# Attention scores of two sequences in one burst, and four instructions moved within a turn

## The reference, cut to what matters

```python
for i in range(DEPTH):                       # 6 layers
    x = attn_layer(shift_tokens(x), ...) + x
    x = ffn_layer(shift_tokens(x), ...) + x
# attn_layer, 16 heads of 64, window 32
q = l2norm(q) * qs; k = l2norm(k) * ksc      # then rotary, with a scale by position
sim = einsum('bhwie,bhwje->bhwij', q, k of own and previous window) * 8
sim = where(mask, -max, sim); attn = softmax(sim)
out = einsum(attn, v); return out @ Wo
# ffn_layer
xn = layernorm(x) * g + bln
a, gate = split(xn @ W1 + b1); return a * gelu(gate) @ W2 + b2
```

## Time and profile before

| | us |
|---|---|
| median of 3 runs | 3596.83 (3594.86 to 3598.45) |
| the profiled execution, its own time | 3596.09 |
| span of its trace | 3594.3 |
| PE busy | 3394.7 (94%) |
| DVE busy | 3151.4 (88%) |
| ACT busy | 2999.4 (83%) |
| POOL busy | 2877.3 (80%) |

### The profile page before, as it was taken

How to read it: one execution, slowest core, us unless ns; L and a number is a source line. 1 busy time by engine, 2 the same in 40 slices (tenths; PEclk the granted TensorE clock), 3 DMA queues, 4 the chain that set the end, 5 groups by cost and what they waited for, 6 DMA issues and landing times.

```text
span 3594.3 us, 92498 instructions
## 1 busy us (share of the span) xinstructions
PE 3394.7 (94%) x29710; PEld 2110.8 (59%) x29710; DVE 3151.4 (88%) x10872; ACT 2999.4 (83%) x8812; POOL 2877.3 (80%) x2383
## 2 busy tenths in 40 slices
PE   7887999999999999999999999999999999999998
PEld 3444656656666666666656666666666656666665
DVE  7998988988988888988988988988988988988986
ACT  6554888888888888888888888888888888888887
POOL 6887887888887888887888887888887888887883
PEclk9998999999999999999999999999999999999999
DMA  5443322333323333322333322333332333332332
GB/s 164 141 133 124 113 99 102 108 115 108 115 101 101 106 112 106 116 103 99 107 115 107 116 102 99 110 116 103 115 106 96 108 118 105 114 106 99 106 103 92
DMA packets 261726, 396.22 MB, mean 110 GB/s; under 512 B 45566, under 2 KB 86588, under 8 KB 261244
## 3 DMA queue, kind: packets, MB, share of 16 engines
q1 hardware_dynamic: 261244, 390.30, 32.4%
HBM read 157.91 MB, written 6.03 MB: 46 GB/s over the span
## 4 chain that ended last, share of the span: by engine, by line
PE 53%; DVE 17%; POOL 14%; issue 7%; ACT 6%; DMA 2%; SPq 1%; DVEq 0%; POOLq 0%; ACTq 0%
PE bank L886 9%; PE bank L875 7%; PE bank L847 6%; PE bank L360 5%; PE bank L362 5%; PE bank L361 5%; DVE ab L1610 4%; PE bank L914 4%; PE bank L829 4%; POOL rot L1359 4%; POOL pr L1345 4%; PE bank L856 4%; DVE wide L1502 3%; PE bank L857 3%; DVE sm L1655 2%
## 5 line engine op out<-in xcount | busy, mean ns | idle before, releaser
L1184 ACT ACTIVATE pr<-sm,nb,rq 128x128 f32<-128x128 f32 (+1 forms) x3072 | 1518.0, 502 | 10.8 <-DVE nb L1661 10.7
L1345 POOL TENSOR_TENSOR pr<-pr,rden 128x640 f32<-128x640 f32 x768 | 966.2, 1258 | 460.1 <-DVE rden L1635 457.7
L1359 POOL TENSOR_TENSOR rot<-ab,swp 128x512 f32<-128x512 f32 x760 | 978.0, 1287 | 74.0 <-DMA swp<-ab 73.4
L1610 DVE TENSOR_TENSOR ab<-bank,ltab 128x1024 f32<-128x1024 f32 x760 | 925.1, 1217 | 80.6 <-PE bank L362 66.7
L1655 DVE CUSTOM_DVE_ANT_0 sm<-bank,mask 128x128 f32<-128x128 f32 (+1 forms) x3072 | 839.4, 328 | 47.5 <-PE bank L847 42.1
L1184 ACT ACTIVATION_READ_ACCUMULATOR pr<-sm,nb,rq 128x1 f32 x3072 | 599.5, 195 | 0.0
L847 PEld LDWEIGHTS bank<-rot 64*64 64x64 f32 x12288 | 288.1, 132 | 436.0 <-issue 364.7
L1365 POOL TENSOR_TENSOR rot<-rot,rkb 128x512 f32<-128x512 f32 x384 | 492.3, 1289 | 64.3 <-DMA rkb<-k_scratch 64.1
L1642 DVE COPY pt<-bank 128x512 f32<-128x512 f32 x768 | 531.3, 692 | 10.2
L875 PE MATMUL bank<-pt,vtok 128*64 128x160 f32 (+1 forms) x6144 | 461.6, 292 | 29.4 <-ACT vtok L1198 29.4
L1172 ACT ACTIVATE sq<-bank 128x512 f32<-128x512 f32 x768 | 452.6, 589 | 43.2 <-DVE ab L1610 19.9
(11 more groups left out here) (213 smaller groups left out, 5743.7 us busy)
## 6 DMA issues: line engine op xcount, KB each, us to landing
swp<-ab SPq DMA_DIRECT2D x1520, 128.0 KB, 2.0
rkb<-k_scratch SPq DMA_DIRECT2D x768, 128.0 KB, 2.9
rot<-c_scratch SPq DMA_DIRECT2D x64, 256.0 KB, 3.3
sq<-c_scratch SPq DMA_DIRECT2D x64, 256.0 KB, 3.3
xs<-xT SPq DMA_DIRECT2D x95, 128.0 KB, 2.3
xs<-xT SPq DMA_DIRECT2D x95, 127.5 KB, 2.4
raw<-Wqkv SPq DMA_DIRECT2D x48, 128.0 KB, 2.7
wo<-Wo SPq DMA_DIRECT2D x6, 512.0 KB, 4.6
```

Of the source, the lines that this page charges most:

```text
L1184: ins = act.activation(pr[:, s % 4, i, t, 0:P + WINDOW * t], sm[:, s % 2, i, cs], ACT.Exp, bias=nb[:, s, t, i:i + 1], scale=head_scale(rq, ...
L1345: ins = pool.tensor_tensor(pr[:, e % 4, :, :, :], pr[:, e % 4, :, :, :], rden[:, e, :, :].rearrange("p t i -> p i t").unsqueeze(3) .to_bro ...
L1359: pool.tensor_tensor(rot[:, PAIRS * (j % 2) + j // 2, :], ab_of(j, 0, lead), swp_of(j, lead), ALU.add).then_inc(qk_rot, 1)
L1610: dve.tensor_tensor(ab_both(j, lead).rearrange("p i (b t) -> p i b t", b=GB), seqs(qk_bank(j, lead)[:, :]).unsqueeze(1).to_broadcast(shape ...
```

## The change

1. `scores` is called in even steps alone and computes both sequences of the head pair in one burst of 16 small matmuls; each sequence has its own 256 columns of banks 0 and 1. The first of the four tiles of a sequence has 64 columns in place of 96. The burst waits for the bias of both sequences of the pair before.
2. PE calls `outputs` right behind `scores`, ahead of the down, output and centring products.
3. DVE takes all maxima of a pair in the even step, in the order: both heads of the first sequence, head 0 of the second, the bias of the first, head 1 of the second. The bias of the second sequence is made in the odd step, ahead of `copy_probs`. The maxima go to the new tile `mx` in SBUF; before they went to spare columns of bank 1.
4. In `copy_probs` one small transpose for two steps of probabilities stands in the even step, and waits for `normalise` of both.
5. Moved in a turn: the layer norm's logarithm and exponential on ACT from step 8 to step 9; `scale_q` of `next` on DVE from 11 to 12; `scale_k` of pair 7 on POOL from 13 to 12; and `a` 0 and `a` 1 exchange their banks (6 and 4).

```diff
@@ tables
- [..., ('prev', 'a', 0, 6), ('next', 'sum', 1, 7), ('prev', 'a', 1, 4)],
+ [..., ('prev', 'a', 0, 4), ('next', 'sum', 1, 7), ('prev', 'a', 1, 6)],
+ 'ln_n': 9,
- 'scale_q': (11, 4),
+ 'scale_q': (12, 4),
-SCALE_STEPS = {13: [('cur', 7)],
+SCALE_STEPS = {12: [('cur', 7)],
-SCORE_TILES = [(0, 0, 0), (1, 32, 32), (2, P, P - WINDOW), (3, P + 64, P + 32)]
+SCORE_TILES = [(0, 64), (32, 96), (P - WINDOW, 96), (P + 32, 96)]
@@ PE
-                def scores(s):
...
-                    if b == 0:
-                        pe.wait_ge(k_norm, scaled)
-                    pe.wait_ge(sc_bias, used)
+                def scores(p):
+
+                    pe.wait_ge(k_norm, n8 + (p + 1))
+                    pe.wait_ge(sc_bias, n16 + 2 * p)
+                    for b in range(GB):
+                        c0 = b * SEQ
+                        for m, (k0, count) in enumerate(SCORE_TILES):
...
-                    if cur is not None:
-                        scores(s)
+                    if s % 2 == 0 and cur is not None:
+                        scores(s // 2)
+                    if s % 2 == 0 and s < 6 and prev is not None:
+                        outputs(s, s // 2 + 5, prev)
+                    if s % 2 == 0 and s >= 6 and cur is not None:
+                        outputs(s, s // 2 - 3, cur)
                     bank_work(s, ("dn", "wo", "rqT", "cen"))
@@ ACT
-                    if s == AT["ln_k"] and (nxt is not None or prev is not None) and kind != "drain":
-                        norms(0, nxt, prev)
+                    if s == AT["ln_k"] and nxt is not None and kind != "drain":
+                        norms(0, nxt, None)
+                    if s == AT["ln_n"] and prev is not None and kind != "drain":
+                        norms(0, None, prev)
@@ DVE
-                    dve.transpose(pt[96:128, e % 4, :, 0, P:P + WINDOW], pr[0:32, e % 4, :, 1, 0:WINDOW])
+                    if e % 2 == 0:
+                        both = slice(e % 4, e % 4 + 2)
+                        dve.wait_ge(p_norm, n16 + (16 * q + e + 2))
+                        dve.transpose(pt[96:128, both, :, 0, P:P + WINDOW], pr[0:32, both, :, 1, 0:WINDOW])
...
+                    if s % 2 and cur is not None:
+                        bias(s)
...
-                    if cur is not None:
-                        maxima(s)
+                    if s % 2 == 0 and cur is not None:
+                        maxima(s, (0, 1))
+                        maxima(s + 1, (0,))
+                        bias(s)
+                        maxima(s + 1, (1,))
```

More of the change, by code:

```diff
@@ L74 @@
  [('prev', 'g', 0, 4), ('next', 'qk', 12, 5)], [('prev', 'g', 1, 6), ('next', 'qk', 13, 5)],
- [('prev', 'g', 2, 7), ('next', 'qk', 14, 5), ('prev', 'a', 0, 6), ('next', 'sum', 1, 7), ('prev', 'a', 1, 4)],
+ [('prev', 'g', 2, 7), ('next', 'qk', 14, 5), ('prev', 'a', 0, 4), ('next', 'sum', 1, 7), ('prev', 'a', 1, 6)],
  [('prev', 'a', 2, 6), ('next', 'qk', 15, 5)]]
@@ L190, in build @@
         nb = sb("nb", [P, STEPS, 2, 2])
+        mx = sb("mx", [P, 2, 2, 2])
         den = sb("den", [P, STEPS, 2, 2])
@@ L203, in build @@
         wide_f = wide[:, :, :].rearrange("p a n -> p (a n)")
-        mx = bank[1][:, UW:UW + 4].rearrange("p (t i) -> p t i", t=2)
         pt_f, pr_f = (t[:, :, :, :, :].rearrange("p a b c d -> p (a b c d)") for t in (pt, pr))
@@ L832, in square_sums @@
                     mm.then_inc(sq_part, 1)
-                def scores(s):
-                    p, b = s // 2, s % 2
-                    scaled = (n8 + (p + 1))
-                    used = (n16 + s)
-                    if b == 0:
-                        pe.wait_ge(k_norm, scaled)
-                    pe.wait_ge(sc_bias, used)
-                    c0 = b * SEQ
-                    for half, c, k0 in SCORE_TILES:
-                        part = slice(64 * (half % 2), 64 * (half % 2) + 64)
-                        for i in range(2):
-                            rows = slice(64 * i, 64 * i + 64)
-                            mm = pe.matmul(bank[i][part, c:c + 96], rot[rows, p, c0 + 64 * half:c0 + 64 * half + 64],
-                                           rot[rows, PAIRS + p, c0 + k0:c0 + k0 + 96], start=True, stop=True)
+                def scores(p):
[4 more added lines that the diff above has]
+                        for m, (k0, count) in enumerate(SCORE_TILES):
+                            part = slice(64 * (m % 2), 64 * (m % 2) + 64)
+                            for i in range(2):
+                                rows = slice(64 * i, 64 * i + 64)
+                                mm = pe.matmul(bank[i][part, c0 + k0:c0 + k0 + count],
+                                               rot[rows, p, c0 + 64 * m:c0 + 64 * m + 64],
+                                               rot[rows, PAIRS + p, c0 + k0:c0 + k0 + count], start=True, stop=True)
                     mm.then_inc(sc_ps, 1)
@@ L973, in turn @@
                         project_out(s - AT["wo"], prev)
-                    if s % 2 == 0 and s < 6 and prev is not None:
-                        outputs(s, s // 2 + 5, prev)
-                    if s % 2 == 0 and s >= 6 and cur is not None:
-                        outputs(s, s // 2 - 3, cur)
                     if s < 3 and prev is not None:
@@ L1660, in maxima @@
                         dve.wait_ge(rq_sb, n2 + (s // 8 + 1))
-                    dve.tensor_tensor(nb[:, s, :, :], mx, head_scale(nrq, p, b), ALU.mult).then_inc(sc_bias, 1)
+                    dve.tensor_tensor(nb[:, s, :, :], mx[:, b, :, :], head_scale(nrq, p, b), ALU.mult).then_inc(sc_bias, 1)
                 def clamp(h, q):
```

17 lines of the change are left out of this document (10 added, 7 removed).

## The result

The changed kernel takes 3717.32 us (median of 4 runs, 3712.45 to 3723.2), the kernel before 3597.64 (4 runs, 3594.86 to 3600.67). The ratio is 1.0334, 95% interval 1.0319 to 1.0350: it is slower by 120 us, where 71 us faster was forecast. The time lies above the range, and beyond the slower rival's 3634.

A forecast was written before the change was run, and what follows sets the result against it. PE was taken to set the pace in part A, ACT's chain in part B. Part A loses 1.52 us a turn, part B stays; over 47 stretches that is 71 us, from 3596.1 to 3525, range 3472 to 3590.

The forecast's parts named there:

- the slower rival: DVE's `copy_probs` late in odd steps, POOL late too: part B +2.3 us, turn +0.8, 3634 us; chance 0.14.
- PE's own work: Joined bursts and fewer changes of array mode cut PE's work by 2.20 us a turn.
- The narrower tile: In a burst's second half, 32 of 384 columns fewer: taken as no gain; 0.34 us if counted in full.
- The rival of a dear second half: A burst's second half costs 0.49 us, not 0.37: 0.92 us a turn left, 3553 us; chance 0.17.
- Part A: Step 14's first `a` product to step 8's sums of squares: PE sets the pace, -1.52 us a turn.
- DVE or ACT now sets the pace in part A too: Sign of a wrong forecast: PE waits appearing in steps 0 to 5.
- Item 1, the exchange of banks: In part B, `a` 0 waits for the first `gelu` instead of the second and starts 0.61 us earlier.
- part B: ACT's first logarithm after step 8's sums to the next `a` product: ACT-bound, unchanged; bounds -1.2 to +2.3 us.
- Item 2, the layer norm's pair: In part B, ACT's chains cost +0.2 us and POOL's `normed` starts 1.2 late; with DVE's reordering, +0.6 together.
- Item 3, DVE's order: In part B, reductions precede bias and odd-step `copy_probs`, up to 1.19 us; with the layer norm's move, +0.6 together.
- The maxima in SBUF: Any difference is hidden by PE's work in part A and small beside DVE's reordering bounds in part B.

The follow-up runs named there:

- the ring: Bursts and DVE's order, no moves, maxima in banks, given a third buffer of masked scores instead of two: ratio 0.9918, 44 us faster than with two.
- the port: The kernel before with only the maxima moved to SBUF, so the bias product reads two SBUF operands: ratio 1.0189, +68 us.
- the centring product: The kernel with bursts, maxima in banks, three buffers and no moves, with `outputs` of step 8 put back behind the centring product: 3547.4 us, ratio 0.9854.

## Why the prediction was wrong, point by point

- **PE's own work.** Right in mechanism and nearly in size. The timeline of the changed kernel:

```profile
2086.82 0.40 PE L363 MATMUL bank<-xl,wqk_h 128*128 128x512 f32 x1
2087.14 0.89 PE L845 MATMUL bank<-rot 64*64 64x64 f32 x32
2087.96 1.20 PE L874 MATMUL bank<-pt,vtok 128*64 128x160 f32 x16
```

  The double burst takes 0.82 to `outputs`; less the first half's 0.49 the second costs 0.33, forecast 0.37, rival 0.49. The narrower tile may have counted after all (0.34 was that bound). The last pass ahead takes 0.32, so going to parts costs its 0.09 to 0.10 once. The estimate worked out from the Trainium skill, TensorEngine Tiling (Array Packing), Instruction Overhead, was 0.40 for the second half; 0.33 is below it. Nor does a floor of 60 columns speak against a gain from 96 to 64 columns, as the prediction had it; no run here parts the tile from the rest. The rival of a dear second half falls.

- **Part A, -1.52 a turn, by "There PE sets the pace".** The step that failed. The starts of PE's sums of squares cut part A in three. Means over the turns between 1000 and 1800 us; the forecast is the prediction's own terms sorted by step:

| | steps 15, 0 | steps 1 to 6 | steps 7, 8 | part A |
|---|---|---|---|---|
| the kernel before | 8.18 | 26.63 | 8.28 | 43.09 |
| forecast change | -0.27 | -0.98 | -0.27 | -1.52 |
| moves undone | 8.37 | 25.46 | 8.50 | 42.33 |
| moves undone, maxima in banks | 8.37 | 25.46 | 8.75 | 42.58 |
| the changed kernel | 9.08 | 25.46 | 8.53 | 43.07 |

  In steps 1 to 6 PE does set the pace, and they lost 1.17, more than forecast, in all three kernels. At both ends the stretch grew instead of shrinking. In the kernel with the moves undone and the maxima in banks, PE's timeline in steps 15 and 7 of one turn has

```profile
1275.11 0.50 PE L359 MATMUL bank<-xh,wqk_h 128*128 128x512 f32 x1 [0.28 <-ACT sq L1169]
...
1307.28 0.30 PE L853 MATMUL bank<-ident,pr 128*128 128x128 f32 x1 [0.60 <-DVE pt L1642]
```

  Without its half burst PE reaches these places earlier, and waits there for ACT's square and for DVE's copy of the probabilities. The prediction read "PE never idles" as slack of the others, but in step 15 that slack was smaller than the 0.49 of a half burst, and in step 7 DVE's new order makes its copy later as well (with maxima and bias in each step PE has no such wait there, and 0.30 for a bias at the next burst). Its last section names the case ("DVE or ACT now sets the pace in part A too"), with no chance of its own. In the changed kernel the wait in step 15 is longer (next point).

- **Item 1, the exchange of banks, "Nothing else waits for that order".** Wrong. The kernel before with the three small moves has part B 0.70 shorter (24.09, against 24.79), more than the 0.61 forecast, but the stretch from the sums of step 14 to those of step 0 is 0.60 longer (8.77 against 8.17). The exchange was run only together with the two moves of `scale_q` and `scale_k`; that it is the one is argued from the place. PE's waits for v's copy and for a square of ACT in that kernel, to be held against the earlier trace rows for the former (before, PE waited 2.4 us for squares):

```profile
PE bank L875 <- ACT vtok L1198: 33.9, 86, 0.6
PE bank L360 <- ACT sq L1172: 19.4, 50, 0.5
```

  What came sooner out of B was waited out behind it, for the square in step 15. In the changed kernel that stretch is 0.90 longer than before, and some turns have another wait in it: `a` 2 of step 15 goes to bank 6 as well, where it now follows `a` 1 directly, and PE waits for DVE's product of that one (L361 for L1683 above, 16.6 us in 19 turns, none before).

- **Item 2, the layer norm's pair.** Mechanism named (POOL's `normed` late, its list dense behind it), size missed: I put 0.2 on the chains and 0.4 on a late copy or `low`, 28 us in all; it cost 46 alone, 75 in the changed kernel and 71 there with banks and a third buffer. PE's wait for v's copy, which was to go, stayed (28.1). POOL waits 92.9 us in 41 turns at `normed`, 2.3 in each and up to 3.1, where I forecast a start late by 1.2 or more. I had no term for PE's wait at bank 6 (24.1 us).

- **Item 3, DVE's order.** Place right: the copy in odd steps, PE waiting up to 2.7 us for L1646. But I counted only reductions moved, "DVE has no more work than before, and is back in phase at each even step". I overlooked that reductions a step early write a buffer a step early. That wait for the exponentials of step s - 1 cost 44 us in the kernel without the moves, where a third buffer gave them back; in the changed kernel it gave nothing.

- **The maxima in SBUF, "small beside the bounds of item 3".** A term put at nothing, and it is about half of the loss: 68 us alone, 65 in the changed kernel, 23 with the ring opened. In the kernel before with the maxima in SBUF, part A grew by 0.18 only, as PE's work hides most of it, but part B by 1.0 (25.81 against 24.79). I had no row with both inputs in SBUF and took the row with one in a bank (0.16) as the price; the bound from above should have been one POOL instruction (1.28) or more, for the input's place was what changed; 2.41 and 3.90 were measured.

- **The rival.** The slower case had its mechanism, a late copy in odd steps with POOL late, and its price in B, 2.3 (measured 2.16). That the two are close is luck: of the 2.16, 1.19 goes when the maxima go back to banks (B is 25.76 then), and the rival had no port in it. Its time was too low because I let part A keep its 1.52, and its chance of 0.14 weighed each cause by itself when they compound.

Settled are the port, the ring, the pair's move and the centring product, each by a run that does or undoes it alone. Read from the traces, and tested by no run, are the waits at the two ends of part A. Argued is the bank exchange apart from the two other small moves, and that the harms compound because they lengthen the same ring.

## What to carry to other kernels

When an operand moves from a bank to SBUF, ask whether the instruction now reads two SBUF tiles while GpSimd works: the price is the rest of what GpSimd has in work, here up to 3.90 us, and the profile shows it as busy time, so look at min and max of the group and not at the waits. When work is done a step earlier, count the buffers that it writes; a ring that was deep enough by one step is not any more. When work is taken from an engine that never idles, that does not tell how much slack the others have: look at each place where it will arrive earlier. And cost edits together if they may lengthen the same ring of engines: on top of the joined bursts the maxima in SBUF cost nothing, the moves 41 us, and both 107.

## What the hardware showed that was not expected

- A 128x4 product of DVE that lasts from 0.13 to 3.90 us with both inputs in SBUF, 0.16 always with one in a bank; in one case it lasted 2.41 us and ended with the second of two POOL products that ran back to back.
- The read of a reduction's accumulator takes 0.08 us to SBUF and 0.14 to a bank.
- After waits of PE of 2.5 to 2.7 us the granted clock fell to 0.50 in five of 12 turns, for some 2 to 4 us, and a pass then took 0.43 instead of 0.23; in the other seven it stayed at 1.00.
- Four one-column products of DVE take 0.49 us where one of four columns takes 0.08 to the next start.
